# Attention stage: output weights split behind the last slot, and unread products on the tensor engine

## What is computed

```python
# x: (8, 256, 512), context: (8, 256, 512), 16 heads of 32; every context row is an "image" row
q = rms_norm(linear(layernorm(x), q_w, q_b), norm_q_w)
k_img = rms_norm(linear(context, k_img_w, k_img_b), norm_k_img_w)
v_img = linear(context, v_img_w, v_img_b)
probs = softmax(q @ k_img.T / sqrt(32))      # per sequence and head
x = x + linear(probs @ v_img, o_w, o_b)
```

## Time and profile before

| | us |
|---|---|
| median of 3 runs | 1544.69 |
| lowest and highest run | 1543.71, 1552.8 |
| span of the profiled execution | 1529.5 |
| first scores of the attention start at | 168.30 |
| last scores of the attention start at | 341.10 |
| first product of route starts at | 353.25 |

### The profile page before, as it was taken

How to read it: one execution, slowest core, us unless ns; L and a number is a source line. 1 busy time by engine, 2 the same in 40 slices (tenths; PEclk the granted TensorE clock), 3 DMA queues, 4 the chain that set the end, 5 groups by cost and what they waited for, 6 DMA issues and landing times.

```text
span 1529.5 us, 37498 instructions
## 1 busy us (share of the span) xinstructions
PE 1409.1 (92%) x8711; PEld 1188.0 (78%) x8712; DVE 1025.9 (67%) x2094; ACT 884.6 (58%) x2022; POOL 607.5 (40%) x699
## 2 busy tenths in 40 slices
PE   7999899998945899999999999999995899999998
PEld 5887656666733788889888888888884678888888
DVE  5555576995778676777677666666656766767742
ACT  5554586993447666766666666666652334444442
POOL 1222386882110422232232233322226777766322
PEclk9999786999955899999999999999997899999999
DMA  6221693001160788878778777778748654444200
GB/s 227 83 83 56 228 367 108 2 2 38 58 254 23 235 278 288 270 271 284 266 264 279 265 264 251 260 258 273 245 154 262 234 173 152 144 132 136 68 14 29
DMA packets 93287, 278.23 MB, mean 182 GB/s; under 512 B 12757, under 2 KB 12886, under 8 KB 92502
## 3 DMA queue, kind: packets, MB, share of 16 engines
q1 hardware_dynamic: 69526, 199.67, 37.2%
q0 software_dynamic: 23680, 77.61, 16.4%
HBM read 209.07 MB, written 76.81 MB: 187 GB/s over the span
## 4 chain that ended last, share of the span: by engine, by line
PE 44%; issue 8%; POOL 4%; DMA 4%; DVE 3%; ACT 2%; ACTq 1%; SPq 1%; DVEq 1%; POOLq 0%
PE m_g L1317 19%; PE m_y L1337 12%; PE f_g L1780 5%; PE m_x L1302 3%; POOL G L1653 2%; PE f_y L1795 2%; POOL hT_low L1659 2%; DMA y_rows<-y 1%; ACT wd_high L1085 1%; DMA raw_d<-in_exp_d 1%; DMA G<-y_rows,slot 1%; DVE X L1835 1%; PE f_sc L1732 1%; PE m_h L1325 1%; PE m_h L1326 1%
## 5 line engine op out<-in xcount | busy, mean ns | idle before, releaser
L1245 POOL DMA_INDIRECT xg<-h_rows,idx x168 | 189.1, 1125 | 452.5 <-PE m_x L1302 443.2
L1317 PE MATMUL m_g<-wgu_high,bxTh 128*128 x660 | 235.5, 357 | 3.9 <-DVE bxTl L1388 3.4
L1317 PE MATMUL m_g<-wgu_low,bxTh 128*128 x660 | 223.2, 338 | 0.0
L1317 PE MATMUL m_g<-wgu_high,bxTl 128*128 x660 | 223.1, 338 | 0.0
L1780 PE MATMUL f_g<-x4T_high,ffn_gu 128*128 128x256 f32 x704 | 174.0, 290 | 3.9 <-DVE x4T_low L1905 3.9
L1090 DVE TENSOR_TENSOR wgu_low<-raw_gu,wgu_high (+1 forms) x64 | 112.5, 1758 | 84.0 <-ACT wgu_high L1080 80.8
L1780 PE MATMUL f_g<-x4T_low,ffn_gu 128*128 128x256 f32 x704 | 167.5, 280 | 0.0
L1388 DVE TENSOR_TENSOR bxTl<-m_x,bxTh 128x512 fp32r<-128x512 f32 x166 | 114.5, 690 | 72.4 <-ACT bxTh L1485 65.1
L1503 ACT ACTIVATE y<-m_y 128x512 f32<-128x512 f32 x164 | 98.2, 599 | 107.5 <-PE m_y L1337 87.1
L635 POOL TENSOR_TENSOR prob<-prob,inv 128x512 f32<-128x512 f32 x128 | 130.3, 1040 | 44.5 <-DVE inv L586 43.2
L1337 PE MATMUL m_y<-wd_high,hidTm 128*128 x328 | 139.8, 426 | 7.8 <-DVE hidTm L1402 5.9
(11 more groups left out here) (270 smaller groups left out, 3284.7 us busy)
## 6 DMA issues: line engine op xcount, KB each, us to landing
raw_gu<-in_exp_gu SPq DMA_DIRECT2D x64, 768.0 KB, 6.6
y_rows<-y SPq DMA_DIRECT2D x164, 256.0 KB, 4.2
raw_d<-in_exp_d SPq DMA_DIRECT2D x64, 512.0 KB, 7.4
y_rows<-zero SPq DMA_DIRECT2D x64, 256.0 KB, 3.3
ffn_gu<-ffn_gu_words SPq DMA_DIRECT2D x1, 5632.0 KB, 23.1
raw_c<-in_ctxT SPq DMA_DIRECT2D x16, 256.0 KB, 2.6
X<-in_x SPq DMA_DIRECT2D x4, 1024.0 KB, 5.5
h_rows<-h SPq DMA_DIRECT2D x16, 256.0 KB, 2.0
```

Of the source, the lines that this page charges most:

```text
L1245: eng.indirect_dma_start(xg[:, u, :].bitcast(F32), None, h_dram, bass.IndirectOffsetOnAxis(ap=idx[half][:, u:u + 1], axis=0)).then_inc(s_g ...
L1317: m = eng.matmul(pg[u % 2][:, 0:2 * I], xT[l][:, u % 2, c, :], W.gu[r][:, buf * DC + c, :], start=c == 0 and n == 0, stop=c == DC - 1 and ...
```

## The change

Four edits, all in `project` and `attend`:

1. At the end of the projection PE makes three products behind each of the last two `turn_q` (`keep_clock(3)`, rounded operands, 512 columns) into `pk`, which nobody reads afterwards.
2. In slots 1, 2, 3 and 4 of the attention PE makes 7, 2, 1 and 1 products of V with itself (f32, 256 columns) into `pO[1]`, before that bank is first used (`FILL`).
3. In slots 65 to 68, behind the last scores, PE makes two such products each into `pS[0]` (`DRAIN`), eight in all.
4. The split of the output weights moves from slots 8 to 15 to slot 65: ACT rounds all four chunks there, DVE makes the rest of two chunks and POOL that of the other two behind its last multiplication.

None of the added products waits on a semaphore or raises one.

```diff
@@ project, tensor engine
+            def keep_clock(times):
+                for n in range(times):
+                    eng.matmul(pk[:, :], Wh[:, 0, 0, 0:P], Wh[:, 0, 0, :], start=True, stop=True)
...
             turn_q(NT - 2)
+            keep_clock(3)
             turn_q(NT - 1)
+            keep_clock(3)
@@ attend
-        HIGHS, LOWS = range(8, 8 + DC), range(12, 12 + DC)
+        HIGHS_AT, DVE_LOWS, POOL_LOWS = SLOTS + 1, range(DC // 2), range(DC // 2, DC)
+        FILL, DRAIN = {1: 7, 2: 2, 3: 1, 4: 1}, 2
@@ attend, tensor engine
+            def keep_clock(times, psum):
+                for n in range(times):
+                    eng.matmul(psum, V[:, 0, 0:P], V[:, 0, 0:S], start=True, stop=True)
...
+                if s in FILL:
+                    keep_clock(FILL[s], pO[1][:, :])
+                if s > SLOTS:
+                    keep_clock(DRAIN, pS[0][:, 0, 0, :])
@@ attend, vector engine
+                if s == HIGHS_AT:
+                    for n in DVE_LOWS:
+                        eng.wait_ge(s_high, n + 1)
+                        eng.tensor_tensor(Wo[1][:, n, :], Wraw[:, n, :], Wo[0][:, n, :].bitcast(F32), ALU.subtract)
@@ attend, scalar engine
-                if s in HIGHS:
+                if s == HIGHS_AT:
                     eng.wait_ge(s_wo, 16)
-                    eng.activation(Wo[0][:, s - HIGHS[0], :], Wraw[:, s - HIGHS[0], :], ACT.Copy).then_inc(s_high, 1)
+                    for n in range(DC):
+                        eng.activation(Wo[0][:, n, :], Wraw[:, n, :], ACT.Copy).then_inc(s_high, 1)
@@ attend, gpsimd
-                if s in LOWS:
-                    c = s - LOWS[0]
-                    eng.wait_ge(s_high, c + 1)
-                    eng.tensor_tensor(Wo[1][:, c, :], Wraw[:, c, :], Wo[0][:, c, :].bitcast(F32), ALU.subtract)
+            for c in POOL_LOWS:
+                eng.wait_ge(s_high, c + 1)
+                eng.tensor_tensor(Wo[1][:, c, :], Wraw[:, c, :], Wo[0][:, c, :].bitcast(F32), ALU.subtract)
```

## The result

The kernel after takes 1530.7 us (median of 20 runs, 1521.4 to 1537.0), the kernel before, run beside it, 1544.4 us (20 runs, 1523.6 to 1553.2). The ratio is 0.9938, 95% interval 0.9919 to 0.9956. Three later comparisons, on three different chips, gave 0.9915 (0.9890 to 0.9940), 0.9921 (0.9891 to 0.9950) and 0.9926 (0.9897 to 0.9956). So the change is worth 0.6 to 0.9%. The medians of the four comparisons differ by 13.7, 14.9, 14.8 and 12.0 us, where 22.5 were forecast. The result lies in the band "within 1%", to which the prediction gave a chance of 0.21.

A forecast was written before the change was run, and what follows sets the result against it. PE was taken as the attention's bound, at half clock in long stretches. Terms -24.1 (attention), +2.35 (drain) and -0.75 (route) sum to -22.5 us: 1544.7 becomes 1522.2 us, 8-in-10 range 1518 to 1532.

The forecast's parts named there:

- the moved split: Attention: taking the split out of slots 8 to 15 saves PE's waits and the second and third half-clock stretches, 14.8 us.
- the first stretch: Attention, 168.6 to 195.9 us at the half clock: the rest of the 24.1 us gain, 9.3 us, comes from it.
- 2 for what differs between runs: Allowance of 2 us for differences between runs, within the forecast's own range of 1518 to 1527 us.
- What bounds it, and the two rates: Attention: PE is the bound; a unit takes 8.25 us at half clock, 4.73 at full, so 0.43 us per us.
- What comes ahead of the first fall: Before the attention's first half-clock stretch: the seam, PE busy 1.09 of 3.4 us, then slot 2's wait of 3.22 us.
- The later falls come from the short waits: Attention: second fall follows a 0.62 us wait for ACT in slot 13, third follows 0.62 and 0.47 us for POOL.
- The waits themselves: Attention: PE's three waits for ACT and POOL, 0.62 + 0.62 + 0.47 = 1.7 us, disappear.
- The fill: Attention start: with unread products slot 2 starts near 173.0, slot 4 at 177.4, slot 63 at 317.0; clock holds over the seam.
- The drain: Attention end: unread products make route start 0.9 to 2.35 us late; the upper bound, 2.35, was taken.
- Route: Route's start: 1.5 us lost at the half clock may be regained; gain 0 to 1.5 us, 0.75 taken.
- What follows keeps its length: Behind the attention: stages keep their length, since the transfers are done long before its end and feed none of its tiles.
- A: Rival: one clock fall remains in slots 4 to 63, costing 11.6 us, so 1533.8 us; chance 0.12.

## Why the prediction was wrong

**The failed step is in the sum**: "Gain 24.1 us, of which 14.8 come from the moved split and the rest, 9.3, from the first stretch". The mechanism, the places and the price per us held. The size of the term did not: it took the 58.0 us at the half clock of one execution as those of every execution. Four profiles hold 58.0, 20.4, 37.6 and 58.0, and give slots of 172.8, 157.4, 164.7 and 172.7 us. Against 148.5 that is a gain of 18.4 us on average, and 16.2 for the profile with the middle clock, not 24.1. Of the two shares the moved split's is the one that failed. Run alone it won 8.4 us, 2 to 9 by its interval, where 14.8 less 1.3 in the drain were due; the products alone won 8.3 where 9.3 were. The median runs agree: on one chip the time at the half clock went from 2 x 0.051 x 1527.6 = 156 us to 2 x 0.0375 x 1512.7 = 113 us. 43 us at 0.41 are 17.6; less the 2.8 of the drain, 14.8. The median span fell by 14.9; the clock is recorded to 0.001 (3 us), and at the 0.32 us per us of these runs the same sum gives 11, so the good match is partly luck. "2 for what differs between runs" was the only allowance, where the stretches alone differ by 15 us.

Stage by stage, means of the four profiles of each kernel: slots 18.4 us shorter, way to route 3.6 longer, route 1.1 shorter, experts 3.1 longer. Together that is 12.8 us shorter, where the medians moved by 12.0 to 14.9. The experts' part is not told from chance: 654.3 to 659.8 us after, 653.3 to 656.8 before.

The warning stood in the text. "The median of the runs is 15.2 us above that span" treats 15.2 us as lying around a span. In every recorded run only 1.7 to 1.9 us lie around it. The profiled execution was thus one of about 1531 us beside a median of 1544.7. It came from faster conditions than the timed runs, by the size of what was later seen between chips (16 us), and it lacks the long way behind the experts (51.2 us, against 69.2 in the first profile of the kernel after). At the same time it came from the dear end of the stretches. So the two first profiles have equal spans by coincidence.

The Trainium skill (TensorE: Matmul & The Clock Gate, Part 1 on the clock gate) warns of something near this: it says that the number of products at the slow clock after the start differs between runs of one kernel. The traces agree, and show it in the middle of a kernel too: at one place, 3.4 to 30.7 us. The prediction took its rule against the change from the same page of the Trainium skill and left this sentence out.

Step by step:

- **What bounds it, and the two rates**: right. 4.73 us per unit in the kernel after, 0.41 us per us at the half clock.
- **What comes ahead of the first fall**: misread. The wait that it names, "3.22 us in which slot 2 waits for the exponentials", stands behind the fall: the clock falls at 168.6, and that wait ends at 173.42. What PE did before it fell is the seam: it waits 0.91 us ahead of the last turn and 1.40 ahead of the first scores. With the six products these two waits are 0.22 and 0.75 us, and the clock holds.
- **The later falls come from the short waits**: right as far as the runs reach, against the rule of the Trainium skill (TensorE: Matmul & The Clock Gate, the section on HAM oscillation), which asks for a longer gap. None of eight profiles without the bunch's waits (four of the kernel after; one each without the drain's products, without the seam's, with the split spread, with the split on POOL) shows a fall between slot 4 and slot 63; with the bunch in slots 40 to 47 the one fall seen moved there. With the split moved and no products, nothing falls behind slot 4 either. What fails is that the waits bring a fall each time, as the sum has it: with the waits and the fill, three of five profiles have none.
- **The waits themselves**, 1.7 us: with the clock up PE is idle for 2.8 us (busy for 149.44 of 152.20), 2.6 of them in six waits instead of the three that were counted, and the slots are 3.7 us longer than without the bunch. In the profile before, the half clock hid a part, and a fourth wait, 0.38 us at 202.61, was not counted.
- **The fill**: right to 0.5 us at slots 2, 4 and 63. That the clock holds over the seam with its six products: right, and without them a fall costs 1.6 us (3.0 forecast).
- **The drain**, +2.35: measured +2.8 in one profile, and +3.9 in the three where the clock falls in it for 3.4 us. The prediction had no such fall in its sum. The upper bound was the right one. Timeline of the kernel after, end of the drain (answers to the earlier trace rows):
```profile
321.82 2.25 ACT L642 ACTIVATE wo_high<-wo_raw 128x512 fp32r<-128x512 f32 x4
...
322.68 1.93 PE L568 MATMUL pO<-probT,V 128*32 128x256 f32 x16
323.62 2.35 DVE L616 TENSOR_TENSOR wo_low<-wo_raw,wo_high 128x512 fp32r<-128x512 f32 x2
323.63 3.48 POOL L660 TENSOR_TENSOR wo_low<-wo_raw,wo_high 128x512 fp32r<-128x512 f32 x2
...
328.85 1.99 PE L575 MATMUL pS<-V 128*128 128x256 f32 x8
...
331.32 1.15 ACT L766 ACTIVATE oT_high<-qT 128x512 fp32r<-128x512 f32 x2 [1.96 <-PEq L61]
```
 PE's last unread product ends at 330.84, and ACT starts route at 331.32, 0.48 later: the seam does wait for products that nobody reads. "The split itself in slot 65 costs nothing there" was wrong by 0.4 us, which with the 2.35 makes the 2.8, and "up to 1 us" without cover was 1.3 (13.5 against 12.2). DVE starts its low parts 7.0 us behind slot 63's scores (6.1 forecast) and ends them 9.3 us behind, where its last copy of the attention was due at 8.8 and stands behind them on its queue. Without the drain's products PE waits 2.18 us for that copy where it waited 0.88 before. With two of them in this wait 0.40 us are left, where the prediction had none. Kernel without the drain's products, then the kernel after (the first of its three new profiles):
```profile
327.48 1.07 PE L568 MATMUL pO<-probT,V 128*32 128x256 f32 x16 [2.18 <-DVE probT L610]
```
```profile
326.62 1.07 PE L568 MATMUL pO<-probT,V 128*32 128x256 f32 x16 [0.40 <-DVE probT L612]
```
- **Route**, -0.75: 147.1, 148.9, 148.8 and 147.7 us, against 148.9 to 149.7 before, 1.1 less on average; the size is right.
- **What follows keeps its length**: right on like chips for the way to the network (51.1 us against 51.2 to 52.7 before); for the experts open, as said above.
- **The rivals**: none came. A asked for one fall in slots 4 to 63, and no profile of the kernel after has one. The case that came, the same mechanism at some 0.6 of its size, was not among them.

## What to carry to other kernels

A profile is one draw. Before a stretch at the low clock is priced as a gain, compare the profiled execution's span and mean clock with the timed runs; where they don't meet, the stretch is a distribution, and its mean belongs in the sum. Put extra work of a side engine one operation at a time where that engine has room, not in a bunch: four in a row made PE wait and let its clock fall, one in six slots on POOL cost nothing, and the same work behind the loop cost 0.4 us under unread products and 1.3 without them. A seam waits for unread products too, so those ahead of it must be weighed against what the clock wins behind it: here six rounded ones won 1.6 us, and the eight of the drain cost 1.5 and brought about 1.2 back.

## What was not expected of the hardware

- Chips differ: the same kernel before has medians of 1525.2, 1528.8 and 1529.3 us on three chips and 1545.0 on a fourth. 17 us of that (68.1 - 51.1) lie in one place, between the experts and the network, where several engines stand idle together (ACT for 8.64 and 3.23 us) and the trace names only "another core or an unknown queue". What they wait for, and whether it belongs to the chip or to what ran beside the kernel, stays open; no run went into it.
- POOL's two low parts take 3.48 us where DVE makes its own two beside them, 1.74 each, against 1.27 in the slots. DVE's first takes 0.68 us and its second 1.76. The Trainium skill (GPSIMD Engine Reference, Specifications) says that POOL shares these interfaces with DVE, with contention where DVE has two inputs from SBUF. The trace agrees: the four operations would take 2 x 0.68 + 2 x 1.27 = 3.9 us one after the other, and take 3.5 side by side.
- The clock came back after 3.4 us where seven dense unread products ran (168.2 to 171.6, one profile), and after 17 or 27 us at the same place with the attention's own work (five profiles). The attention's own work doesn't fix the time: behind the later waits it took 3.4 to 27.3 us.
